# Side chunks in parts, at new places of both slot kinds, in a pipelined attention kernel

## What is computed

```python
NL, D, H, DFF = (6, 256, 16, 1024)        # 16 heads of 16 features; B, L = 4, 512
def _attn(q, k, v, mask):
    scores = jnp.einsum('bqhd,bkhd->bhqk', q, k) / np.float32(np.sqrt(HD))
    scores = jnp.where(mask[:, None, None, :], jnp.float32(-jnp.inf), scores)
    w = jax.nn.softmax(scores, axis=-1)
    return jnp.einsum('bhqk,bkhd->bqhd', w, v)
for i in range(NL):
    xn = _adaln(x, noise_emb, n1_w[i], n1_b[i])
    q, k, v = jnp.split(xn @ qkv_w[i].T, 3, axis=-1)
    a = _attn(_rope(q), _rope(k), v, src_mask) @ so_w[i].T      # heads split and joined
    x = x + a
    xn = _adaln(x, noise_emb, n2_w[i], n2_b[i])
    a = _attn(_rope(xn @ cq_w[i].T), _rope(context @ ck_w[i].T), context @ cv_w[i].T, ctx_mask) @ co_w[i].T
    x = x + a
    xn = _adaln(x, noise_emb, n3_w[i], n3_b[i])
    h = jax.nn.gelu(xn @ f1_w[i].T + f1_b[i], approximate=False)
    x = x + (h @ f2_w[i].T + f2_b[i])
```

## Time and profile before

| | us |
|---|---|
| median of 3 runs | 4208.83 (4204.97 to 4214.45) |
| the profiled execution, its time | 4208.19 |
| its span, first to last instruction | 4206.5 |
| TensorE busy | 3796.9 (90%) |
| VectorE busy | 2806.2 (67%) |
| ScalarE busy | 2493.6 (59%) |
| GpSimd busy | 1114.0 (26%) |

### The profile page before, as it was taken

How to read it: one execution, slowest core, us unless ns; L and a number is a source line. 1 busy time by engine, 2 the same in 40 slices (tenths; PEclk the granted TensorE clock), 3 DMA queues, 4 the chain that set the end, 5 groups by cost and what they waited for, 6 DMA issues and landing times. The chain is left out here.

```text
span 4206.5 us, 52946 instructions
## 1 busy us (share of the span) xinstructions
PE 3796.9 (90%) x19478; PEld 1695.6 (40%) x19478; DVE 2806.2 (67%) x4476; ACT 2493.6 (59%) x4206; POOL 1114.0 (26%) x992
## 2 busy tenths in 40 slices
PE   3899999999999999999999999999999999997558
PEld 1233344433444433444423444433444433443346
DVE  5778766688766678766678766687766677652311
ACT  1577665677655676655667656677656576654112
POOL 3332322232222233222233222233222233200043
PEclk7999999999999999999999999999999999998779
DMA  5555533355533365433365433365433365411245
GB/s 141 128 145 137 133 75 72 78 147 139 127 72 73 79 154 139 117 72 75 80 151 139 117 72 80 80 151 139 112 74 77 87 166 142 114 43 47 74 105 113
DMA packets 281874, 448.72 MB, mean 107 GB/s; under 512 B 50632, under 2 KB 190032, under 8 KB 281296
## 3 DMA queue, kind: packets, MB, share of 16 engines
q1 hardware_dynamic: 237456, 380.61, 37.4%
q0 software_dynamic: 44160, 64.73, 6.3%
HBM read 278.54 MB, written 172.24 MB: 107 GB/s over the span
## 5 line engine op out<-in xcount | busy, mean ns | idle before, releaser
L872 ACT ACTIVATE prob<-ps 128x512 f32<-128x512 f32 x3072 | 1749.5, 595 | 1165.2 <-PE ps L797 1162.8
L1027 DVE TENSOR_REDUCE negmax<-ps 128x2 f32<-128x1024 f32 x1536 | 1815.7, 1217 | 490.3 <-PE ps L824 490.0
L797 PE MATMUL ps<-qstack,kstack 114*128 114x512 bf16 x3072 | 1133.7, 390 | 78.6 <-ACT prob L872 42.5
L810 PE MATMUL psv<-prob,v 128*32 128x512 f32 x6144 | 835.1, 616 | 0.0
L797 PEld LDWEIGHTS ps<-qstack,kstack 114*128 114x128 bf16 x3072 | 273.2, 97 | 1212.9 <-ACT prob L872 885.7
L824 PE MATMUL ps<-kstack,qstack 49*128 49x512 bf16 x3072 | 488.4, 386 | 92.1 <-DVE negmax L1027 74.6
L647 POOL DMA_DIRECT2D qstack<-mrow x192 | 107.5, 561 | 1246.0 <-ACT mrow L933 1245.8
L772 PE MATMUL side<-nT,wf 128*128 128x256 f32 x1536 | 373.3, 386 | 14.6 <-DVE hT L1063 7.9
L783 PE MATMUL side<-wf,hT 128*128 128x256 f32 x1536 | 349.5, 380 | 3.3 <-DVE hT L1063 1.7
L1063 DVE TENSOR_SCALAR hT<-side,f1b 128x256 f32<-128x256 f32 x384 | 167.5, 478 | 248.2 <-PE side L772 248.1
L772 PEld LDWEIGHTS side<-nT,wf 128*128 128x128 f32 x1536 | 289.0, 192 | 65.5 <-DVE hT L1063 20.6
(11 more groups left out here) (169 smaller groups left out, 3439.9 us busy)
## 6 DMA issues: line engine op xcount, KB each, us to landing
bounce<-parts SPq DMA_DIRECT2D x288, 256.0 KB, 2.5
qstack<-bounce SPq DMA_DIRECT2D x384, 192.0 KB, 5.7
kstack<-bounce SPq DMA_DIRECT2D x384, 192.0 KB, 6.2
value_sums<-osum SPq DMA_DIRECT2D x192, 256.0 KB, 6.7
bounce<-low SPq DMA_DIRECT2D x96, 256.0 KB, 2.1
hT<-value_sums POOLq DMA_DIRECT2D x96, 256.0 KB, 4.8
nT<-inverse POOLq DMA_DIRECT2D x96, 256.0 KB, 3.8
ctxT<-in_ctxT SPq DMA_DIRECT2D x24, 512.0 KB, 4.6
```

Source lines behind the costliest of these rows:

```text
L797: nc.tensor.matmul(ps2[:, n % RING2, :], kk[0:ROWS, h, kt * P:(kt + 1) * P], q[0:ROWS, h, :], start=True, stop=True).then_inc(s_p2full, 1)
L810: mm = nc.tensor.matmul(psv[32 * i:32 * i + 32, 0, :], v[j % 2][:, kt, (HD + 1) * h:(HD + 1) * h + 32], prob[:, 4 * (u % 2) + i, :], start ...
L872: nc.scalar.activation(prob[:, 4 * (u % 2) + i, :], ps2[:, n % RING2, :], ACT.Exp, scale=HD ** -0.5).then_inc(s_prob, 1)
L1027: nc.vector.tensor_reduce(out_at, ps1[:, 2 * (n % 2):2 * (n % 2) + 2, :], AX, ALU.max, negate=True).then_inc(s_p1free, 1)
```

## The change

A chunk may now have several places, and then runs in as many equal parts: its list of matmuls is cut (`steps_of`), the first part waits for the bank, the last one reports it filled, and the engines that read the chunk do so at the place of the last part. No matmul, eviction or transfer is added or removed. O's chunk 0 of the short slot runs in four parts at places 17, 18, 19 and 19, its chunk 1 in two at 21 and 25, HK's chunk 1 in two at 13 and 14. HV's chunk 0 of the long slot runs in four parts at 1, 2, 2 and 3. All other chunks stay whole, many at other places. The plan sorts later parts ahead of new chunks within one place.

```diff
 SHORT = {
-    "M": [25, 0], "HV": [1, 3], "HT": [6, 7], "HQ": [8, 9], "HK": [12, 14], "O": [18, 20],
-    "SPLIT": (12, 14, 18, 20), "PARTS": 23, "RECIP": 6, "NORM": (10, 11),
-    "LN_HT": dict(stats=[0, 0, 1, 1], aggregate=1, guess=2, newton=3, tiles=[3, 3, 4, 4]),
+    "M": [28, 0], "HV": [(1,), (2,)], "HT": [(5,), (6,)], "HQ": [(7,), (9,)], "HK": [(11,), (13, 14)],
+    "O": [(17, 18, 19, 19), (21, 25)], "SPLIT": (12, 14, 18, 20), "PARTS": 20, "RECIP": 5, "NORM": (13, 15),
+    "LN_HT": dict(stats=[0, 1, 1, 1], aggregate=1, guess=1, newton=2, tiles=[2, 2, 3, 3]),
 }
 LONG = {
-    "M": [27, 0], "HV": [1, 3], "HT": [6, 7], "HQ": [8, 9], "O": [11, 12], "HK": [13, 15], "LT": [16, 17],
-    "F1": [18, 19, 20, 21, 22, 23, 24, 25], "F2": [26, 28, 30, 31],
-    "SPLIT": (13, 15, 18, 20), "GELU": (22, 26), "PARTS": 24, "RECIP": 5, "NORM": (8, 9),
-    "LN_HT": dict(stats=[0, 0, 1, 1], aggregate=1, guess=2, newton=3, tiles=[3, 3, 4, 4]),
+    "M": [26, 0], "HV": [(1, 2, 2, 3), (4,)], "HT": [(6,), (7,)], "HQ": [(8,), (9,)], "O": [(11,), (12,)],
+    "HK": [(13,), (14,)], "LT": [(17,), (17,)], "F1": [(18,), (19,), (20,), (21,), (22,), (23,), (24,), (25,)],
+    "F2": [(27,), (28,), (29,), (30,)], "SPLIT": (13, 17, 19, 24), "GELU": (23, 28), "PARTS": 22, "RECIP": 5,
+    "NORM": (8, 9), "LN_HT": dict(stats=[0, 1, 1, 1], aggregate=3, guess=3, newton=4, tiles=[4, 4, 4, 5]),
     "LN_LT": dict(stats=[12, 12, 12, 12], aggregate=13, guess=14, newton=14, tiles=[14, 14, 15, 15]),
 }
...
             def put(*names):
                 for name in names:
-                    for c, at in enumerate(places[name]):
-                        plan[at].append((name, c))
+                    for c, ats in enumerate(places[name]):
+                        for part, at in enumerate(ats):
+                            plan[at].append((name, c, part, len(ats)))
...
+            for at in plan:
+                plan[at].sort(key=lambda chunk: chunk[2] == 0)
...
-            def begin(k, what, c):
+            def begin(k, what, c, part=0):
 
                 n = number[(k, what, c)]
-                if n >= 1:
+                if n >= 1 and part == 0:
                     pe.wait_ge(s_read, n)
                 return side[:, 0, :]
+
+            def steps_of(n, part, parts_of):
+                return range(n * part // parts_of, n * (part + 1) // parts_of)
+
+            def filled(mm, part, parts_of):
+                if part == parts_of - 1:
+                    mm.then_inc(s_full, 1)
...
-            def project_T(bank, w, act_T, m):
-
-                for k in range(KD):
+            def project_T(bank, w, act_T, m, part, parts_of):
+
+                for k in steps_of(KD, part, parts_of):
                     mm = nc.tensor.matmul(bank, w[:, k, m * P:(m + 1) * P], act_T[:, k, :], start=(k == 0), stop=(k == KD - 1))
-                mm.then_inc(s_full, 1)
+                filled(mm, part, parts_of)
...
-                    both = any(what in ("HQ", "HK", "O", "F1", "F2") for what, c in plan[2 * u])
+                    both = any(what in ("HQ", "HK", "O", "F1", "F2") and part == parts_of - 1
+                               for what, c, part, parts_of in plan[2 * u])
```

More of the change, by code:

```diff
@@ L727, in side_work @@
                     i = ("HQ", "HK", "HV").index(what)
[L728 removed]
+                    if i == 0 and c == 0 and part == 0:
                         wait_read(pe, k, "HT", 0)
@@ L763, in side_work @@
                     th, cc = divmod(c, 4)
-                    if c == 0:
+                    if c == 0 and part == 0:
                         wait_read(pe, k, "LT", 0)
@@ L828, in head0 @@
             def head0():
-                for what, c in slot_chunks(-1)[0]:
-                    side_work(-1, what, c)
+                for chunk in slot_chunks(-1)[0]:
+                    side_work(-1, *chunk)
                 pe.wait_ge(s_vones, 2)
@@ L843, in slot @@
                         pass2(k - 1, u, 1)
-                    for what, c in plan[2 * u]:
-                        side_work(k, what, c)
+                    for chunk in plan[2 * u]:
+                        side_work(k, *chunk)
                     if p2:
@@ L854, in slot @@
                         pass2(k - 1, u, 3)
-                    for what, c in plan[2 * u + 1]:
-                        side_work(k, what, c)
+                    for chunk in plan[2 * u + 1]:
+                        side_work(k, *chunk)
             run_slots(head0, slot)
@@ L1112, in slot @@
                         maximum(k, at)
-                    for what, c in plan[at]:
-                        side_work(k, what, c)
+                    for what, c, part, parts_of in plan[at]:
+                        if part == parts_of - 1:
+                            side_work(k, what, c)
                     if p1 and at == places["PARTS"]:
```

73 lines of the change are left out of this document (39 added, 34 removed).

## The result

| | us, median (lowest to highest) |
|---|---|
| kernel before, measured beside the changed one | 4209.56 (4204.97 to 4214.45) |
| changed kernel | 4153.04 (4149.47 to 4156.07) |
| ratio | 0.9866 [0.9852, 0.988] |
| forecast | 4094, range 4050 to 4145 |

The change is 1.3% faster, so the sign was right, but the time lies 8 us outside the range. The profiled execution has a span of 4149.3 us against 4206.5, 57.2 less; the forecast had 114.

What follows compares the result with a forecast made beforehand. TensorE with its waits bounds the kernel: 5.4 us of waits per short slot, 7.8 per long. 24 short slots x 1.9 = 46 and 22 long x 3.2 = 70 off 4208.2, plus 2 at the start: 4094 us, range 4050 to 4145.

Steps and rivals of the forecast that it cites:

- The long slot: Long slots 6 to 47: waits removed by new places, 3.2 us less each (2.0 to 4.0), list of places to 90.6.
- the wait between the transposes: Long slot, place 17: second transposes wait for ScalarE's read of the first, 1.5 us.
- the wait behind the first gelu: Long slot, gelu at 23: TensorE waits 1.3 us for 0.83 before, +0.5 us.
- the 5.0 us that I put to lateness in places 16 to 18: Long slot before: waiting transposes, a late first-pass matmul ahead and a late chunk behind lose 5.0 us.
- The short slot's work alone, 58.9: Short slot, TensorE: 57.5 us without waits, 1.1 for bare units, 0.3 for late maxima, sum 58.9.
- 0.8 a multiply: Short slot, VectorE: each normalising multiply, moved from places 10 and 11 to 13 and 15, takes 0.8 us.
- The end of the short slot, 60.9: Short slot's end: shift rows land with the loads' drain at 60.0 to 60.5; with scatter 60.9, gain counted 1.9.
- the landing stays 6.9 us behind the issue: Rival, chance 0.12: short slots stay at 62.8 to 63.0, only long ones gain, 4140 us.
- long slot short of its gain: Rival, chance 0.10: VectorE or ScalarE later than counted in the long slot, gain 1.2 us each, 4138 us.
- The start: Slots 0 and 1: bare ends, later shift rows cost up to 3 us once; put at +2 us.
- Nothing net: Rival, chance 0.04: landing holds every short slot, long slot gives its gain back at 17 and 23, 4205 us.
- slower: Rival, chance 0.06: shift rows landing after 10.2 us set the short slot, 3.6 us more each, 4226 us.

Runs made afterwards that it cites:

- e8: Changed kernel with M chunk 0 at place 22, O's second chunk at 20 and 21, first multiply at place 8, all in the short slot: 4073.1 us, ratio 0.9683.
- e2: New place numbers for the short slots only, long slots as in the kernel before: 4230.1 us, ratio to before 1.0042.
- e4: Changed kernel with the short slot's first normalising multiply at place 8 instead of 13: 4143.9 us, ratio to before 0.9838.
- e5: Changed kernel with the short slot's M chunk 0 (shift rows) at place 22 instead of 28, O's second chunk at 20 and 21: 4084.8 us, ratio 0.9708.
- e11: e8 with O's second chunk of the short slot in four parts at 24, 26, 28 and 30 instead of two at 20 and 21: 4070.4 us, ratio 0.9656.
- e6: Changed kernel with four added, unused matmuls into the side bank at place 31 of each short slot: 4156.2 us, ratio to before 0.9876.

## Why the forecast was wrong, step by step

- **The long slot: right.** -3.2 each was forecast, by the list of places to 90.6; the undisturbed long slots take 90.59. The terms hold singly: the wait between the transposes 1.41 (1.5), the wait behind the first gelu 1.13 (1.3), nothing behind the second. On average 90.90, since some of those that follow a short slot begin at the lower clock and take 92.1. 63 us for 70. But one cause was missed: part of the 5.0 us that I put to lateness in places 16 to 18 was the clock, 0.50 in 3097.50 to 3100.90. It went with the wait that caused it, so the sum came out.
- **The short slot's work alone, 58.9: 0.8 too low.** Without the wait and the clock fall it is 4.77 + 28.12 + 8.39 + 16.91 + 1.54 = 59.7. By the forecast's prices places 16 to 19 take 7.5 (two units of 2.62, a chunk of 1.73, 0.27 for a bare unit, 0.3 of lateness), so all of the difference lies there: the step "0.8 a multiply" took its price from a place where GpSimd's operation was nearly through and moved the multiply to one where 1.4 us of a longer one were left. It costs 1.91.
- **The end of the short slot, 60.9 against a measured 63.2: the step that failed.** The forecast read the landing as tied to the drain of the loads, 14.7 us behind the low part of K, and put it at 60.0 to 60.5. The direction was right: the issue moved 2.6 us later and the landing by 0.2. The size was off at three terms. The low part of K ended at 46.3, not 45.4 (+0.9); the multiply is a part of that, shown by e8, where it ends at 45.8, and the rest is open. On average the slot's start lost 0.9 at the lower clock, which shifts everything behind it (+0.9). And I took the drain itself as the landing, while the shift row lands 1.0 after the last store on average: 5.2 us after its issue instead of 60.25 - 56.1 = 4.15 (+1.0). Most of this is the 11 slots with the late landing (1.8 on average, against 0.3 in the others), and in 8 of them the instruction packet, which the forecast had nowhere. Together 2.8, from which comes off the 0.65 that I had added to the landing as scatter: 2.2 of the 2.3 us missed, x 24 = 52 us, and with the 7 of the long slots the 59 between 4094 and 4153.
- **The clock was not in the sum at all.** The earlier trace rows had shown it, 0.98 in long slots against 1.00 in short ones, and I read it as "the 2.4 GHz level". The question that a 2% lower mean should have raised is which stretch is at half, and whether the wait before it stays, goes or moves. That wait went, and others came at the short slots' ends.
- **The rivals.** By the number, "the landing stays 6.9 us behind the issue" (4140) and "long slot short of its gain" (4138) lie nearest, but neither is what happened: the time to landing shrank by 2.3 us, and the long slot gave its gain. The short slots of 62.8 to 63.0 that the first of them promised were met by chance, from a landing that hardly moved at all. The case between it and the forecast, that the row lands with the drain but the drain is later, belonged in the forecast's own spread, which stopped at 61.5. A landing at 63.1 gives 4094 + 24 x 2.2 = 4147.
- **The start: +3 for +2**, and the part behind slot 48 2 us shorter for none.
- **Nothing net, slower:** no. But e2 shows that the short table alone is slower by 0.42% [0.26, 0.57]: the landing does set the short slot, as the slower rival said, at 0.3 us per slot instead of 3.6 (7 us); as much comes from the long slots behind them (94.04 for 93.76) and from the start (slot 1 begins 8.5 later and is 3.0 shorter).

## To carry over

When a step is moved, price it at its new neighbours, above all an operation of VectorE with two operands in SBUF that comes to stand beside one of GpSimd. When a small transfer is awaited, list everything that is queued ahead of it, stores too, and ask whether it can be issued ahead of them: here moving it six places earlier was worth 68 us, more than the 46 that I had expected of the whole short table. And read the granted clock by stretch, not by slot, since a wait that moves takes its clock fall along; in this kernel such a wait cost its length and then 1.5 us more in most cases, 1.8 on average. Last, when a part of a chunk is moved away, look whether it covered a copy of ScalarE (places 15 and 21 here), not only whether its unit becomes bare.

## What the runs showed of the hardware that I had not expected

- A VectorE multiply of 128x512 with two operands in SBUF takes 0.68 us alone and ends 0.55 to 0.56 us after the GpSimd operation beside which it started: 1.91 us in the change, 1.37 in e4, 0.86 in the kernel before, in all 24 short slots of each. By its end it looks as if it waited until GpSimd was through and then ran most of its own time. The Trainium skill ("SBUF — State Buffer", SBUF: two separate sides) describes the port pair that the two engines share as held by one operation to its end while the other blocks; these rows agree with it.
- A wait of TensorE of 2.07 us, in a stream that is dense on both sides, was followed by a stretch at 0.50 (before, long slot 39), waits of 2.89 and 2.99 us too, one of 1.18 us was not. Length alone does not tell: over all traces the shortest wait at a slot's start that was followed by the lower level is 1.36 us (before), the longest that was not is 2.47 (e4). At the lower level the eight products with the values took 1.94 us instead of 1.06. Filling 1.72 us of such waits with useless matmuls was worth 16 us over the kernel.
- The same 8 KB transfer took 1.9 us to land with nothing queued, 4.2 on average when issued 0.2 us behind the first of the eight loads (e5), 7.0 to 7.5 behind all of them. In e8 the second row goes out at 48.4 us of the slot, 0.25 behind the first load, and takes 4.3; in e11 it goes out at 47.6, 0.9 ahead of the first load, and takes 1.9.
- A matmul of 512 columns of fp32 takes 0.86 us (3.44 / 4) and is two records of the trace (the four of e6 are the x8 of its row).
- A 16 KB packet of the instruction queue takes 1.0 to 1.1 us, and in 8 of 24 short slots of the changed kernel a shift row's last packets came through only at its end.
